# Seventeen full-array products that nobody reads, set into TensorE's waits of one turn and of the closing normalisation

## The reference

```
x = x + quantised(val * gelu(gate)) @ down.T          # layer 0, on rms-normalised rows
x = x + up(relu(down(x)))                             # layer 1, weights generated per sequence
x = x + alpha * attention(ada_rmsnorm(x))             # layer 2, 16 heads of width 16
x = x + alpha * swiglu(ada_rmsnorm(x))
x = layernorm(x) * weight + bias + tanh(cond) ...     # layer 3
```

## Time and profile before

| | us |
|---|---|
| runs (3) | 1058.87, 1060.81, 1067.25 |
| median | 1060.81 |
| profiled execution, its own time | 1060.28 |
| its span | 1058.2 |
| mean granted clock of TensorE | 0.987 |
| busy: PE / DVE / ACT / POOL | 1021.9 / 762.4 / 628.1 / 223.9 |

### The profile page before, as it was taken

How to read it: one execution, slowest core, us unless ns; L and a number is a source line. 1 busy time by engine, 2 the same in 40 slices (tenths; PEclk the granted TensorE clock), 3 DMA queues, 4 the chain that set the end, 5 groups by cost and what they waited for, 6 DMA issues and landing times.

```text
span 1058.2 us, 16466 instructions
## 1 busy us (share of the span) xinstructions
PE 1021.9 (97%) x5369; PEld 633.7 (60%) x5369; DVE 762.4 (72%) x1197; ACT 628.1 (59%) x852; POOL 223.9 (21%) x217
## 2 busy tenths in 40 slices
PE   7999999999999999999999999999999899999996
PEld 6776677778544343444444443433468678888884
DVE  5766667887876678787787868778855476667754
ACT  5456323352366678777777877767763545555555
POOL 1000001121231223333333424121202221212211
PEclk9899999999999799999999999999999999999998
DMA  9967634125525263444446353553210000000001
GB/s 288 364 194 238 156 115 119 32 40 150 131 96 130 47 204 75 159 102 133 126 96 179 78 168 85 160 128 88 91 48 10 1 21 20 20 20 0 21 20 40
DMA packets 92040, 110.93 MB, mean 105 GB/s; under 512 B 47184, under 2 KB 57424, under 8 KB 90960
## 3 DMA queue, kind: packets, MB, share of 16 engines
q1 hardware_dynamic: 60736, 100.56, 32.2%
q10 hardware_dynamic: 31248, 9.65, 5.0%
HBM read 65.81 MB, written 33.03 MB: 93 GB/s over the span
## 4 chain that ended last, share of the span: by engine, by line
PE 69%; DVE 10%; ACT 5%; issue 4%; DMA 1%; ACTq 1%; POOL 1%; DVEq 0%; SPq 0%; POOLq 0%
PE st_ps L1771 14%; PE st_ps L1627 10%; PE av_ps L1609 8%; PE mx_ps L1771 7%; PE val_ps L1484 5%; PE gate_ps L1484 5%; DVE mx L1201 5%; PE misc_ps L1540 4%; PE misc_ps L1647 3%; PE mx_ps L1564 3%; PE misc_ps L1660 3%; PE y_ps L1494 2%; DVE stage L1210 2%; PE misc_ps L1651 1%; PE misc_ps L1686 1%
## 5 line engine op out<-in xcount | busy, mean ns | idle before, releaser
L1201 DVE TENSOR_REDUCE mx<-mx_ps 128x1 f32<-128x512 f32 x488 | 314.6, 684 | 105.8 <-PE mx_ps L1564 103.8
L1564 PE MATMUL mx_ps<-kring,qring 48*128 48x512 f32 x500 | 202.1, 466 | 4.0 <-DVE mx L1201 1.9
L1627 PE MATMUL st_ps<-qring,kring 50*128 50x512 f32 x512 | 188.8, 449 | 3.2 <-ACT shared L926 3.2
L1627 PEld LDWEIGHTS st_ps<-qring,kring 50*128 50x128 f32 x512 | 77.4, 187 | 148.9 <-issue 115.9
L926 ACT ACTIVATE pbuf<-st_ps 128x1024 f32<-128x1024 f32 x128 | 129.2, 1023 | 46.5 <-PE st_ps L1627 45.1
L926 ACT ACTIVATE shared<-st_ps 128x1024 f32<-128x1024 f32 x128 | 128.2, 1021 | 39.7 <-PE st_ps L1627 38.6
L1564 PEld LDWEIGHTS mx_ps<-kring,qring 48*128 48x128 f32 x500 | 85.6, 186 | 31.4 <-DVE mx L1201 26.1
L1047 ACT ACTIVATE p_hi<-shared 128x512 fp32r<-128x512 f32 x64 | 40.4, 632 | 90.5 <-DVE shared L1378 88.4
L1383 DVE TENSOR_TENSOR p_lo<-shared,p_hi 128x512 fp32r<-128x512 f32 x64 | 52.8, 825 | 47.2 <-ACT p_hi L1047 47.2
L1378 DVE TENSOR_TENSOR shared<-st_ps,shared 128x512 f32<-128x512 f32 x64 | 44.0, 687 | 47.3 <-PE st_ps L1771 19.6
L1264 DVE SCALAR_TENSOR_TENSOR h<-val_ps,r,gelu 128x1024 f32<-128x1024 f32 x32 | 41.0, 1283 | 48.2 <-PE val_ps L1484 48.2
(11 more groups left out here) (234 smaller groups left out, 2087.7 us busy)
## 6 DMA issues: line engine op xcount, KB each, us to landing
chunk<-in_gen_w SPq DMA_DIRECT2D x8, 2048.0 KB, 8.1
qring<-q_parts SPq DMA_DIRECT2D x64, 192.0 KB, 3.5
kring<-k_parts SPq DMA_DIRECT2D x64, 192.0 KB, 4.6
q_parts<-stage SPq DMA_DIRECT2D x16, 512.0 KB, 2.9
k_parts<-stage SPq DMA_DIRECT2D x16, 512.0 KB, 2.8
xres<-in_xT SPq DMA_DIRECT2D x8, 512.0 KB, 11.5
shared<-in_x SPq DMA_DIRECT2D x8, 512.0 KB, 12.3
q_parts<-stage SPq DMA_DIRECT2D x16, 256.0 KB, 3.0
```

What stands on the lines that cost most here:

```text
L1201: nc.vector.tensor_reduce(mx[h // GH % 2][:, col:col + 1], mx_ps[:, qt % 2], AX, ALU.max).then_inc(S["mx_free"], 1)
L1564: nc.tensor.matmul(out, qring[h // GH][r:r + QROWS, h % GH // 2, qt * P:(qt + 1) * P], kring[h // GH][r:r + QROWS, h % GH // 2, :], start= ...
L1627: ins = nc.tensor.matmul(st_ps[half][:, kt % 2], kring[g][r:r + SROWS, i % GH // 2, kt * P:(kt + 1) * P], qring[g][r:r + SROWS, i % GH // ...
```

## The change

It adds 17 products of the full array (float32r, 128 stationary columns, 512 moving columns) in five places and moves nothing. Two come behind the scores of step 11 of turn 1 and four behind the first half's scores of step 12, ahead of its value products. They write `misc_ps` and wait for the second addition of VectorE to `xres` (`x2`). Six come ahead of the first average of the closing normalisation, one behind that average, and four behind the second; they write a bank of `mx_ps`, whose last reader is the last Silu.

```diff
@@ step() of TensorE @@
+                def unread(times):
+
+                    wait(pe, "x2", KD * (a + 1))
+                    keep_busy(misc[:], w_hi["q"][:, 0, 0:P], w_hi["q"][:].rearrange("p k n -> p (k n)"), times)
+
                 for half in range(2):
                     if has_b:
                         wait(pe, "exp", 2 * (NH * b + i) + half - 1)
...
                     if has_b:
                         ins.then_inc(S["st_ready"], 1)
+                    if isinstance(j, int) and (j, i, half) == (1, 11, 1):
+                        unread(2)
+                    if isinstance(j, int) and (j, i, half) == (1, 12, 0):
+                        unread(4)
                     if half < len(cuts) and has_av:
                         weigh_values(*cuts[half])
@@ the closing normalisation of TensorE @@
             wait(pe, "oaug", NG * NB)
+            wait_ffn(pe, "silu", KF * NB)
+            idle = gate_hi[:, 0, 0:P], gate_hi[:, 0, 0:L]
+            keep_busy(fgate_ps[0], *idle, 6)
             for hh, cs in halves:
                 wait_ffn(pe, "added", 2 * NB - 1 + hh)
                 nc.tensor.matmul(stat[hh][:, cs], mean_w[:], xsum[:, cs], start=True, stop=True)                     .then_inc(F["stat"], 1)
+                keep_busy(fgate_ps[0], *idle, (1, 4)[hh])
             for hh, cs in halves:
```

## The result

| | before | changed |
|---|---|---|
| median | 1059.19 us (20 runs, 1052.70 to 1067.25) | 1054.16 us (20 runs, 1052.23 to 1063.05) |
| runs below 1056 us | 6 of 20 | 16 of 20 |
| profiled execution: time, span, mean clock | 1060.28, 1058.2, 0.987 | 1054.46, 1052.7, 0.996 |

The ratio is 0.9954, with a 95% interval from 0.9933 to 0.9976: 0.5% faster, and the interval leaves out 1. (A ratio here is worked out over all runs and need not be the quotient of the two medians.) The spread is to be read beside the median: both kernels have executions at 1052 to 1053 us, but the kernel before reaches them rarely.

The account below looks back on a forecast made before the run. It took TensorE at low clock after waits as the bound in turn 1. 1060.28 - 5.1 (turn 1) - 0.4 (closing) = 1054.8, given as 1054.9 us; own range 1052.6 to 1056.8, widened with two rivals to 1052.4 to 1061.0.

Parts of the forecast that it names:

- The clock in turn 1: Turn 1, steps 12 to 15: products in the wait keep TensorE at full clock, gaining 5.1 us.
- The replay: Turn 1 from step 12, retimed at full clock with VectorE setting the pace: turn 2 at 353.05 instead of 358.16.
- half of the low stretch: Turn 1, upper bound on the clock gain: 6.8 of 13.6 us, if all of it were TensorE's.
- The price of the products: Turn 1: step 11's two are covered, cost taken as 0; step 12's four make the value products 0.28 us late.
- The closing normalisation: At the kernel's end: added products hold the clock and shorten the averages, gain 0.4 us, between -0.3 and 0.9.
- rival 1: Turn 1 and closing: the products change nothing in the clock, as the skill's rule has it; 1060.6 us, chance 0.09.
- Rival 2: The clock holds in turn 1 but falls in a later stretch, at a price of 5.1 us; 1060.0 us, chance 0.10.
- Rival 3: Step 12 of turn 1 and closing: low clock comes first, products take 0.43 us each; +2.3, 1062.6 us, chance 0.05.
- The sum: Whole kernel: the profiled 1060.28 us less 5.1 in turn 1 and 0.4 at the end, 1054.8 us.

Follow-up runs that it names:

- e1: The change with its six products in turn 1 only, without the closing eleven: 1056.06 us, ratio 0.9990 to the kernel before.
- e4: The change's six products in turn 1 only, on 48 rows of the array instead of 128: 1054.75 us, ratio 0.9978 to the kernel before.
- e5: The change with only the four products in step 12 of turn 1: 1054.56 us, ratio 0.9971 to the kernel before.
- e7: The change with eight products in place of four in step 12, none in the closing normalisation: 1057.11 us, ratio 0.9971 to the kernel before.
- e11: The change without the two products in step 11, closing eleven kept: 1052.71 us, ratio 0.9950 to the kernel before.
- e2: The change with its eleven closing products only, turn 1 as before: 1057.69 us, ratio 1.0004 to the kernel before.
- e6: The change with only the two products in step 11 of turn 1: 1056.32 us, ratio 0.9989 to the kernel before.
- e3: The change's six products in turn 1 moved behind the waits, no closing eleven: 1057.85 us, ratio 1.0001 to the kernel before.
- e8: The full change plus two more products in turn 1 step 1 and two in turn 8: 1053.40 us, ratio 0.9943 to the kernel before.
- e9: The full change run again unaltered: 1055.06 us, ratio 0.9969 to the kernel before.
- e10: The full change plus two products between steps 10 and 11 of turn 8: 1054.74 us, ratio 0.9957 to the kernel before.

## Why the prediction was right, point by point

**The clock in turn 1.** The step held: products in the wait keep 1.00 behind it, as the changed kernel, e1, e4, e5, e7 to e11 show, while e2 (none), e6 (only two, in the gap before) and e3 (all behind it) fall. Predicted 5.1 us, measured 5.07. The replay's stations agree: with the 0.45 us added to the changed kernel's times, the value products were expected at 341.32 and came at 341.31, step 14 at 347.3 and 347.30, turn 2 at 353.05 and 353.09. The replay was right that VectorE holds TensorE up in step 13: its first maxima product waits 0.33 us for a reduction (343.12); half of the low stretch, 6.8 us, would have been too much.

**The price of the products.** The four stand 0.27 us in the way (0.28 predicted); the two move a score that the wait for VectorE covers, at no cost (e11 against the change: 64.1 us each for turn 1).

**The closing normalisation.** Predicted 0.4, measured 0.45 us.

**The rule on long gaps (rival 1).** It would have given no gain. The clock fell with a longest gap of 0.78 us, and filling it kept the clock: here the trace decides against the rule in "TensorE: Matmul & The Clock Gate" of the Trainium skill, section "Why this matters for your kernels", as the whole of the matter. The prediction's argument against this rival, that both falls follow TensorE about half busy, was weaker than it looked. In e7 TensorE was busy for 2.60 of the 3.20 us ahead of its fall in turn 8, no less than the 2.50 of 3.20 us around the same wait with which the kernel before kept its clock:

```profile
748.30:751.50 3.20, 2.60 (x13) 0.95 (x14) 1.65 (x3) 2.58 (x4) 2.34 (x1) 0.99 0.07 19
```

So the share of busy time does not decide against the rival; that filling the wait kept the clock does.

**Rival 2, a fall elsewhere.** It does happen. Falls at 294 to 297 us are in e1, e2, e3, e6, e8, e9 and e10, two of which have turn 1's wait as before; falls at 751 to 755 us are in e3 and e7. The falls at 294 to 297 us come ahead of the first product of the change at 338 us (e8 alone adds any sooner), so the change cannot have brought them. For turn 8 two falls, one with turn 1 at full clock and one without, only suggest the same. The prediction priced such a fall at 5.1 us; the traces give about 1.3 us for the one in turn 8 (e7), 2.4 us for a fall of 6.8 us in turn 1 (e1) and 8.0 for one of 20.5 us (e8: 72.1 against 64.1).

**Rival 3, slower.** Its mechanism is real (0.43 us for each product once the clock has fallen, e3), its place is not reached in the change, since the products come before the fall.

**The time.** 1054.9 predicted, 1054.16 measured. Part of this closeness is luck. The sum starts from one execution of 1060.28 us, and the median of 20 runs of before came out at 1059.19, 1.1 us lower. The 0.5 us by which the first three runs' median lay above that execution would have made the sum 1055.3; the prediction gave 1054.9 without saying why. The profiled executions differ by 5.8 us (1060.28 and 1054.46; 5.5 between their spans), of which 0.45 us was there before the change began and 0.4 us was lost again between turn 2 and the feed-forward part's end, where the prediction saw nothing. The execution that the sum starts from had the fall in turn 1. Most executions of the kernel before have one like it or as costly: of the 29 beside e9, 18 have a mean clock of 0.985 to 0.989 and take 1056.6 to 1062.6 us, and the one of 1053.2 us has 0.995. That the median fell by 5.0 us and not by 5.5 would go with the few that had not fallen; this link is argued from the mean clocks, since only the profiled runs leave a trace that tells the place.

## What to carry to other kernels

Where a stretch at the low clock follows waits of TensorE of under a microsecond each, put products that nobody reads into the wait itself, as many as fit before what TensorE waits for is ready: here four ahead of the value products were enough, though they came 0.27 us in the way, two in the gap before did not do, and each of the four more that eight have cost its 0.23 us. Replay the stretch at full clock from the same work elsewhere in the trace, with the engine that becomes the bound, before claiming half of the low stretch. And compare distributions: an edit like this takes away one of several falls that come and go between executions, so its gain shows in how many of them are slow.

## What the runs showed of the hardware that was not expected

- The same program ran in 1052.7 to 1068.4 us, and its time goes with the mean granted clock: 1053.2 us at 0.995, 1059.1 at 0.987 or 0.988, 1068.4 at 0.978.
- A fall behind turn 1's wait lasted 13.7 us in two traces (before, e6) and 6.8 in two (e2, e3); the lengths seen anywhere but at the end were 3.4, 6.8, 13.7 and 20.5 us.
- The clock also fell where TensorE's bars were nearly full: 6.75 of 6.80 us in e1, step 0 and the start of step 1 of turn 1. The kernel before runs the same instructions there, its bars fill 6.74 of the same 6.80 us, and its clock stayed at 1.00:

```profile
289.50:296.30 6.80, 6.74 (x22) 3.10 (x22) 5.01 (x8) 3.22 (x4) 2.52 (x3) 1.00 0.27 52
```

  So the busy share of the bars does not tell whether the clock falls there; what decides stays open. Six products on 48 rows held the clock in step 12 (e4), and one full product more in two places of step 1 did not (e8).
